# Finer messages, finer one-hots and a wait by a loaded count in a graph attention layer

## What is computed

```python
h = (x @ W).reshape(N, H, C)                      # N = 3125, H = 4, C = 64
a_src = jnp.sum(h * att_src[None], axis=-1)
a_dst = jnp.sum(h * att_dst[None], axis=-1)
alpha = leaky_relu(a_src[src] + a_dst[dst], 0.2)  # edges and self loops
m = segment_max(alpha, dst)
alpha = exp(alpha - m[dst])
denom = segment_sum(alpha, dst)
msg = h[src] * (alpha / (denom[dst] + 1e-16))[:, :, None]
out = relu(segment_sum(msg, dst).reshape(N, H * C) + bias)
```

## Time and profile before

| | us |
|---|---|
| median of 3 runs | 2297.5 |
| lowest, highest | 2290.2, 2309.3 |
| the profiled execution | 2303.08 |
| its span | 2301.3 |

### The profile page before, as it was taken

How to read it: one execution, slowest core, us unless ns; L and a number is a source line. 1 busy time by engine, 2 the same in 40 slices (tenths; PEclk the granted TensorE clock), 3 DMA queues, 4 the chain that set the end, 5 groups by cost and what they waited for, 6 DMA issues and landing times.

```text
span 2301.3 us, 27576 instructions
## 1 busy us (share of the span) xinstructions
PE 1508.8 (66%) x7534; PEld 991.1 (43%) x7535; DVE 1088.9 (47%) x2637; ACT 515.5 (22%) x1098; POOL 750.6 (33%) x803
## 2 busy tenths in 40 slices
PE   2457777799999699915246667475766543099960
PEld 1423333356666456714123334233433333099950
DVE  5698989955414631190325445344443663022223
ACT  0234444510000122201012323232323010032210
POOL 5000000024334000004767778776730612600026
PEclk8678989999999899957567878777888755599985
DMA  8000000000020000002433333333310011366644
GB/s 263 7 0 0 0 0 0 0 1 1 5 64 1 25 25 0 1 5 61 116 88 88 90 90 88 89 91 84 85 41 19 0 55 48 109 205 214 212 151 128
DMA packets 98561, 146.75 MB, mean 64 GB/s; under 512 B 15536, under 2 KB 66513, under 8 KB 98324
## 3 DMA queue, kind: packets, MB, share of 16 engines
q0 software_dynamic: 26528, 69.57, 10.8%
q1 hardware_dynamic: 56692, 46.45, 6.8%
q10 hardware_dynamic: 15232, 29.36, 3.6%
HBM read 116.56 MB, written 28.76 MB: 63 GB/s over the span
## 4 chain that ended last, share of the span: by engine, by line
PE 56%; issue 16%; DVE 12%; another core or an unknown queue 5%; ACT 4%; POOL 4%; DMA 1%; ACTq 1%; DVEq 0%; SPq 0%; POOLq 0%
PE ps L1172 11%; PE ps L1041 9%; PE ps L994 5%; PE ps L1251 4%; PE ps L1265 4%; PE ps L1107 4%; PE ps L1096 4%; PE ps L1171 4%; PE ps L991 3%; POOL xs L738 2%; ACT mem L793 2%; POOL mem L747 2%; DVE mem L1430 1%; ACT mem L856 1%
## 5 line engine op out<-in xcount | busy, mean ns | idle before, releaser
L721 POOL DMA_INDIRECT mem<-table,mem x391 | 437.6, 1119 | 157.4 <-issue 111.4
L1172 PE MATMUL ps<-mem 128*128 x832 | 339.0, 503 | 0.0
L688 POOL TENSOR_SCALAR mem<-mem 128x128 f32<-128x128 f32 x156 | 105.1, 688 | 585.2 <-ACT mem L795 420.1
L1171 PE MATMUL ps<-mem 128*128 128x264 bf16 x416 | 136.6, 328 | 212.2 <-issue 135.7
L856 ACT ACTIVATE mem<-ps x416 | 162.8, 391 | 444.9 <-PE ps L1172 271.8
L994 PE MATMUL ps<-mem 128*128 128x400 bf16 x816 | 230.8, 368 | 0.0
L1041 PE MATMUL ps<-mem 128*128 128x384 bf16 x1300 | 226.5, 330 | 4.4 <-DMA mem<-L_gnn_b_dram 3.5
L991 PE MATMUL ps<-mem 128*128 128x400 bf16 x408 | 151.5, 371 | 113.4 <-DVE mem L1430 41.8
L793 ACT ACTIVATE mem<-ps x204 | 170.8, 837 | 204.5 <-PE ps L994 176.3
L1430 DVE TENSOR_SCALAR mem<-mem 128x400 bf16<-128x400 f16 x816 | 207.7, 318 | 0.0
L1171 PEld LDWEIGHTS ps<-mem 128*128 128x128 bf16 x416 | 42.8, 103 | 331.3 <-issue 320.4
(11 more groups left out here) (397 smaller groups left out, 2024.7 us busy)
## 6 DMA issues: line engine op xcount, KB each, us to landing
mem<-L_ffn_W_dram ACTq DMA_DIRECT2D x56, 512.0 KB, 4.2
xs<-mem SPq DMA_DIRECT2D x2, 3584.0 KB
mem<-xs SPq DMA_DIRECT2D x56, 128.0 KB, 3.2
ys<-mem SPq DMA_DIRECT2D x56, 128.0 KB, 2.3
mem<-table,mem POOLq DMA_INDIRECT x395
mem<-x_dram SPq DMA_DIRECT2D x8, 640.0 KB, 7.3
mem<-L_ffn_W_dram SPq DMA_DIRECT2D x4, 1024.0 KB, 6.6
table<-mem SPq DMA_DIRECT2D x6, 528.0 KB
```

Of the source, the lines that this page charges most:

```text
L721: pool.indirect_dma_start(ring[:, t % RING, :], None, table3[:, :], bass.IndirectOffsetOnAxis(ap=IDX[:, t:t + 1], axis=0)).then_inc(row_in ...
L1171: pe.matmul(flat[:, bass.ds(clear, ROW)], zeroG[:, 0:P], zeroG[:, :], start=True, stop=False, skip_group_check=True)
L1172: pe.matmul(flat[:, bass.ds(bank, ROW)], OH[:, q % 2, s, :], ringW[:, bass.ds(slot, ROW)], start=False, stop=False, skip_group_check=True) ...
```

## The change

The messages go from four tiles an instruction to one, so that `msg_ready` counts tiles. The one-hots go from eight steps an instruction to two, and TensorE waits for them at every second step. At every fourth step (`PACE`) TensorE loads one value into a register from a new row 64 of `RG2`, which holds the tile's number of each step plus 1, taken for the last of the four steps, and waits until `msg_ready` has reached that value. The row is written by one more VectorE instruction in the plan. The order of work on each engine, the buffers and the gathers stay as they are. All of the diff that does something:

```diff
             def steps(q):
                 for n, row in enumerate((0, 32, 33)):
                     pe.load(step_regs[n], RG2[row:row + 1, q * CHK:(q + 1) * CHK])
-                pe.wait_ge(hot_ready, q + 1)
                 for s in range(CHK):
...
-                    if s % QT == 0:
-                        pe.wait_ge(msg_ready, min(k // QT + 1, QUADS))
+                    if s % 2 == 0:
+                        pe.wait_ge(hot_ready, k // 2 + 1)
+                    if s % PACE == 0:
+                        pe.wait_ge(msg_ready, pe.value_load(RG2[64:65, k + PACE - 1:k + PACE], min_val=1, max_val=ET))
...
+            ch.mark(dve.tensor_scalar(RG2[64:65, :], ps[64:65, 4, 0:STEPS], 1.0, None, ALU.add))
...
             def hots(q):
                 if q >= 2:
                     dve.wait_ge(st_ps, (q - 1) * CHK)
-                dve.tensor_tensor(OH[:, q % 2, :, :], iotaC[:, :].unsqueeze(1).broadcast_to([P, CHK, P]),
-                                  DLOC[:, q * CHK:(q + 1) * CHK].unsqueeze(2).broadcast_to([P, CHK, P]), ALU.is_equal).then_inc(hot_ready, 1)
+                for s in range(0, CHK, 2):
+                    dve.tensor_tensor(OH[:, q % 2, s:s + 2, :], iotaC[:, :].unsqueeze(1).broadcast_to([P, 2, P]),
+                                      DLOC[:, q * CHK + s:q * CHK + s + 2].unsqueeze(2).broadcast_to([P, 2, P]), ALU.is_equal).then_inc(hot_ready, 1)
...
             def messages(b):
                 dve.wait_ge(exp_ready, b + 1)
-                for t in range(b * BT, min(b * BT + BT, QUADS * QT), QT):
-                    rows = ring[:, t % RING:t % RING + QT, :]
-                    m = rows[:, :, 0:D].rearrange("p k (n c) -> p k n c", c=HC)
-                    dve.tensor_tensor(m, m, rows[:, :, D:D + HEADS].unsqueeze(3).broadcast_to([P, QT, HEADS, HC]), ALU.mult).then_inc(msg_ready, 1)
+                for t in range(b * BT, min(b * BT + BT, ET)):
+                    m = ring[:, t % RING, 0:D].rearrange("p (n c) -> p n c", c=HC)
+                    dve.tensor_tensor(m, m, ring[:, t % RING, D:D + HEADS].unsqueeze(2).broadcast_to([P, HEADS, HC]), ALU.mult).then_inc(msg_ready, 1)
```

## The result

| | before, us | changed kernel, us | ratio, 95% interval |
|---|---|---|---|
| first comparison | 2295.1 | 2374.9 (2372.7 to 2377.8) | 1.0335, 1.0295 to 1.0375 |
| second, with `r_change` | 2311.8 | 2363.6 | 1.0227, 1.0185 to 1.0270 |
| third, with `r3_change` | 2311.4 | 2365.3 | 1.0227, 1.0168 to 1.0285 |

The change costs 52 to 80 us, and the forecast of 2326 us and its range up to 2355 us were both too low. In all there are six comparisons, the last five on five different chips.

The account below looks back on a forecast made before the run. The prediction took TensorE, with its register-load holes, to bound the step loop. Its terms, 32 + 3 + 0 + 0 - 7 + 0.5 = 28.5 us, took the median of 2297.5 to 2326 us; range for 8 in 10: 2274 to 2355.

Parts of the forecast that it names:

- What bounds the kernel: Step loop: TensorE holds it, with 1.84 us holes behind `logit_rows` made of three register loads before each eight steps.
- The removed waits: TensorE's waits for messages and one-hots: an earlier first one buys nothing; costed at 0, at most 12 us.
- Part 1, the load's length: TensorE's one-value load: 0.59 us, 0.65 with surroundings; exposed at each eight's first step, 32 us plus 3 for short instructions.
- Part 1, the cover of the fifth step: Load before each eight's fifth step: hidden by the wait for ScalarE's copy; 0, or 34 us if uncovered.
- Rival C: Chance 0.13: first half, the fifth step's load is exposed too; second half, TensorE's granted clock falls; 28 + 34 us, 2360.
- Part 2, the short operations: VectorE's shorter messages and one-hots: 25 us more work, but early wherever needed; cost 0, 25 us if uncovered.
- rival A: Chance 0.32: stalls last until GpSimd's lead is used up, so GpSimd paces and only the tail pays 7 to 10 us.
- Part 3, GpSimd: Gathers held up less by shorter VectorE operations, mostly becoming waiting for TensorE: 7 us off, bounds 0 and 52.
- rival B: Chance 0.15: GpSimd paces the loop and its gathers speed up; 2258 us in full, 2278 with half the effect.
- The sum: Whole kernel: 32 + 3 + 0 + 0 - 7 + 0.5 = 28.5 us slower.

Follow-up runs that it names:

- r_change: The changed kernel run again beside the kernel before: 2363.6 us against 2311.8, ratio 1.0227.
- r3_change: The changed kernel run once more beside the kernel before: 2365.3 us against 2311.4, ratio 1.0227.
- p1_prefetch: Kernel before, with the next eight steps' register loads issued between the present steps into a second register set: 2281.5 us against 2311.8.
- e2c_loads: Kernel before plus only the 104 value loads, result unused, and the plan's new row: 2348.0 us against 2311.4.
- e3_fourth_load: Changed kernel, counts taken by a fourth load of eight values instead of two single ones: 2366.9 us, kernel before 2311.8.
- e1c_short: Changed kernel with a constant in place of the loaded count, so short messages and one-hots without loads: 2347.0 us, kernel before 2311.4.
- e6_load_first: Kernel before plus an unused value load at the first step of each eight only: 2239.1 us against 2238.8.
- s2_long_loud: Kernel before with long operations, plus empty VectorE instructions giving as many semaphore increments as the change: 2236.5 us against 2238.3.
- s1b_short_quiet: Kernel before with short messages and one-hots, but its own increments and waits: 2342.3 us against 2299.7.
- p2_prefetch_short: Kernel before with early register loads into a second register set plus short messages and one-hots, constant waits: 2326.9 us against 2311.8.
- e1b_short: Changed kernel with a constant in place of the loaded count, in another comparison: 2208.6 us, kernel before 2238.3.
- t1_short_lead: Kernel before with GpSimd kept 12 steps closer to TensorE: 2287.5 us against 2299.7, ratio 0.9938.

## Why the prediction was wrong, point by point

- **What bounds the kernel.** Right for the comparison of the profile. The hole behind `logit_rows` is made of register loads, and `p1_prefetch` shows it by taking it away: 30 us. What was missing is that the kernel stands close to a second bound, the gathers, which sets the pace in the comparisons at 2239 us.
- **The removed waits.** Right: a message is waited for 5.5 us, 2 times, instead of 6.8 us, 4 times; costed at 0 with at most 12 us. No trace shows a gain by an earlier message.
- **Part 1, the load's length.** The row that I took it from was wrong, and the sum came out too low all the same. I took 0.59 us from the load of eight values, with the floor of about 0.6 us that the Trainium skill gives ("DMA: Bandwidth & Descriptors", section "Latency and other measured facts") beside it; the load of one value takes 0.30 to 0.49 us, so here the measurement decides against that floor. What I left out are the instructions that `value_load` adds for its bounds, 0.17 and 0.02 us, and the gaps around them. I costed 0.71 us for each first step, register wait included. The gaps before it grew by 1.07 us in the tail, 1.05 in `e2c_loads`, which doesn't even wait against the register. Fifty-two of them would be 55 us instead of 37 us; over the whole loop, where stalls fall into these gaps too, `e2c_loads` has 43 us more of them.
- **Part 1, the cover of the fifth step.** Right. The gap grew by 0.14 us in the tail. Over the loop it grew by 0.71 us on average, and by 0.29 us in `e2c_loads`, but that is not the load: `e3_fourth_load` has no load there, the same median gap and the same time.
- **Rival C's second half** came true with the first load: the granted clock fell from 0.76 to 0.69 in the gather stretch and from 0.88 to 0.84 in the tail. In `e2c_loads` it is 0.70 and 0.84, in `e1c_short` 0.73 and 0.90, and only the former has slower products. The longer hole at the head has the larger part in it: at 2239 us a pass takes 513 ns with the first load alone (`e6_load_first`), 497 with the fifth's alone and 486 with none (`s2_long_loud`). I had left the clock out of the sum. Loads alone: 32 + 3 us forecast, 37 us measured at 2311 us. That fit is luck: by the table the loop grew by 43 us of first gaps and 22 us of slower ordinary gaps, less 21 us of shorter stalls. C's total, 62 us, is also the nearest of all cases to the 52 to 80 us measured, although its first half, the exposed second load, didn't come true.
- **Part 2, the short operations.** This is the step that failed. I gave them 0, with 25 us as the price "if that cover were gone". They cost 36 us alone (`e1c_short`), 45 us beside early loads, and 17 us beside the loads of the change (2365.3 - 2348.0, two medians whose single runs just touch). The cover is not gone: VectorE holds nothing up (in `e1c_short` TensorE waits for L1675 and L1706 5.2 and 3.4 us). Where they stand alone, stalls come in its place, a term that my sum didn't have, although showed one and rival A named it: late copies of 199 us (202 in `s1b_short_quiet`) against 164, and beside early loads 288 in `p2_prefetch_short` against 235 in `p1_prefetch`. Beside the loads of the change the late copies are not longer (117 and 124 against 125); the 17 us stand in the first gaps (240 against 223), and why is open.
- **Part 3, GpSimd.** Right in kind and inside its bounds of 0 and 52 us: the gathers' mean is 1122 ns in the profile of the changed kernel, where a few take up to 4.5 us, but 1017 ns in `r3_change` and 1057 in both `e1b_short` and `e1c_short`, and the wait for TensorE grew, as forecast. I took 7 us off. At 2239 us the short operations gain 28 to 34 us, between rival B's half and full effect (20 and 40 us); at 2311 us nothing is gained, because GpSimd isn't the one waited for.
- **Rival A** is right in kind about the loads at 2239 us (3 and 4 us, under its 7 to 10) and wrong at 2311 us. Its premise, that the stalls end when GpSimd's lead is used up, has only `t1_short_lead` for it, and there only for a third of them.
- **The sum.** 28.5 us stood for 73 us between the profiled executions and 52 and 54 us in the two later comparisons. In the last of these it can be taken apart: 35.5 us forecast for the loads and the plan, 37 measured; -7 us forecast for the short operations (Parts 2 and 3), +17 measured beside the loads. So the missing 25 us are almost all in the short operations. In the first comparison, which lost 80 us, no half was run, and how its further 26 us divide is not known.

What stays open. Why TensorE's completions come late in some comparisons and not in others isn't settled. Each of the five chips on record had one comparison, so a lasting property of the chip can't be told from one of the occasion, and the kernel before has no trace at 2239 us. That shorter operations without the loads make the kernel slower there is measured, and their traces have longer stalls; that they do it by letting GpSimd issue more densely is only argued (a shorter lead helped by 12 us, which fits, but it changes more than density). In the two comparisons at 2239 us the whole change was never among the kernels, so that it would be faster there is only suggested by its halves. And `p1_prefetch`, which beats both kernels where it ran, wasn't tried there.

## What to carry to other kernels

Take a register load for what stands around it too: cost its bounds and the gaps between its instructions (here 1.05 us for a load of 0.40) and a lower clock behind the longer hole, keep it out of the hole at the head of a group, and issue it into a second set of registers while the present group runs (30 us here). Making operations finer gains only if somebody waits for them; otherwise look at what their new rhythm does to the engine beside them and to whoever is already stalling. And where two engines stand close to the same pace, the same edit can win in one comparison and lose in the next: measure a change whole and its parts in one comparison before adding up.

## What the runs showed that I had not expected

- The same kernel takes 2238 to 2239 us in two comparisons and 2295 to 2312 us in four. It goes with late completions in the loop: absent in the traces of the first kind, 56 to 208 us of ScalarE's waiting in those of the second. Stalls also take the place of holes: `p1_prefetch` has 154.6 us of such waiting, 40 times, more than the kernel before. Its first gaps are 77 us shorter, its gaps inside the eights 53 us longer, and it is 30 us faster.
- Short operations of VectorE have both signs: ratios of 0.984 to 0.988 in the first kind, 1.015 to 1.018 in the second, in the same kernels.
- A load of 0.40 us makes the products behind it slower: 554 ns a pass against 503, at a granted clock of 0.70 against 0.76 while rows are gathered.
- One register's load takes 0.30 to 0.49 us against 0.59 for eight, but in a bounded `value_load` it lengthens TensorE's hole by 1.05 us, more than a whole load of eight values.
